# Attention over heads of 16: tiles taken three at a time on rings of three PSUM banks, two banks per instruction

## The reference

```python
x_n = layer_norm(x)
q, k, v = x_n @ Wq + bq, src @ Wk + bk, src @ Wv + bv   # src: x_n or the context
s = einsum('bqhd,bkhd->bhqk', q, k) * 16 ** -0.5 (+ mask)
x = x + (softmax(s) @ v).reshape(b, n, 256) @ Wo + bo
```

## Time and profile before

| what | value |
|---|---|
| median of 3 runs | 4270.73 us (4268.64 to 4275.31) |
| profiled execution, its time and span | 4268.74 us, 4267.0 us |
| PE busy (modelled) | 3949.2 us, 93% |
| DVE, ACT, POOL busy | 2756.7 us (65%), 2414.2 us (57%), 1660.3 us (39%) |
| mean granted clock of PE | 0.944 |
| rough places of the stages, us | SELF0 to 660, CROSS0 to 1110, MLP0 to 1400, CROSS1 to 1860, SELF2 to 2455, CROSS2 to 2960, MLP2 to 3250, SELF3 to the end |

### The profile page before, as it was taken

One profiled execution on the slowest core, in us unless ns is written; L12 is line 12 of the kernel. 1 busy time (PEld: TensorE's weight loads), 2 busy tenths in 40 slices (PEclk: granted clock), 3 DMA queues, 4 the chain that ended last, 5 costly groups with the idle time before them and its releaser, 6 DMA issues. The chain is left out here.

```text
span 4267.0 us, 64410 instructions
## 1 busy us (share of the span) xinstructions
PE 3949.2 (93%) x20562; PEld 1985.0 (47%) x20562; DVE 2756.7 (65%) x6815; ACT 2414.2 (57%) x5093; POOL 1660.3 (39%) x1661
## 2 busy tenths in 40 slices
PE   6988999999796999999999999997988999999998
PEld 3333343333485343333333333432874555555555
DVE  3555568777365777789999978873653444444443
ACT  2444446767431566778888767774324554554553
POOL 2323322111232022137777722211326665666664
PEclk7888889999797899999999999997999999999999
DMA  4434335544001445444444355541000000000000
GB/s 94 85 61 70 62 65 105 82 82 69 24 1 26 103 79 83 76 72 85 61 62 61 57 98 86 81 77 46 1 25 6 6 11 12 11 1 12 11 6 10
DMA packets 135498, 220.30 MB, mean 52 GB/s; under 512 B 42736, under 2 KB 45168, under 8 KB 133488
## 3 DMA queue, kind: packets, MB, share of 16 engines
q1 hardware_dynamic: 135152, 216.02, 28.5%
HBM read 59.69 MB, written 5.51 MB: 15 GB/s over the span
## 5 line engine op out<-in xcount | busy, mean ns | idle before, releaser
L998 ACT ACTIVATE Pr<-ST 128x512 f32<-128x512 f32 (+3 forms) x2220 | 1157.1, 560 | 787.8 <-PE ST L547 774.0
L547 PE MATMUL ST<-stk 50*128 50x512 f32 (+3 forms) x2560 | 1006.6, 456 | 104.5 <-ACT Pr L998 75.8
L1211 DVE TENSOR_REDUCE mx<-MX 128x1 f32<-128x512 f32 x1056 | 701.3, 682 | 259.2 <-PE MX L547 257.1
L547 PE MATMUL MX<-stk 48*128 48x512 f32 (+3 forms) x1760 | 735.1, 455 | 27.6 <-issue 13.6
L1607 POOL TENSOR_SCALAR Pr<-Pr,mx 128x128 f32<-128x128 f32 (+3 forms) x512 | 549.6, 1086 | 388.9 <-DVE mx L1375 388.9
L547 PE MATMUL OV<-Pr,V 128*32 128x512 f32 (+3 forms) x4784 | 633.7, 603 | 2.9 <-ACT Pr L998 1.5
L547 PEld LDWEIGHTS MX<-stk 48*128 48x128 f32 x1760 | 313.5, 192 | 563.6 <-DVE mx L1211 257.1
L547 PEld LDWEIGHTS ST<-stk 50*128 50x128 f32 x2560 | 422.4, 191 | 286.7 <-ACT Pr L998 214.0
L1486 POOL CAST mhl<-mx 128x16 fp32r<-128x16 f32 x160 | 32.1, 201 | 899.2 <-DVE mx L1211 860.6
L1211 DVE TENSOR_REDUCE mx<-OV 128x1 f32<-128x512 f32 x480 | 327.4, 682 | 59.3 <-PE OV L547 58.3
L547 PE MATMUL OV<-stk 48*128 48x512 f32 (+3 forms) x800 | 355.3, 444 | 0.1
(11 more groups left out here) (154 smaller groups left out, 7464.9 us busy)
## 6 DMA issues: line engine op xcount, KB each, us to landing
stk<-hi SPq DMA_DIRECT2D x640, 128.0 KB, 4.8
stk<-lo SPq DMA_DIRECT2D x320, 128.0 KB, 5.4
misc<-misc SPq DMA_DIRECT2D x160, 128.0 KB
sums<-spread SPq DMA_DIRECT2D x80, 256.0 KB
misc<-in_ctx_t SPq DMA_DIRECT2D x24, 512.0 KB, 6.9
W_even<-in_w SPq DMA_DIRECT2D x4, 1024.0 KB, 5.2
W_even<-in_w SPq DMA_DIRECT2D x2, 2048.0 KB, 9.7
XH<-in_ctx_rows SPq DMA_DIRECT2D x8, 512.0 KB, 3.8
```

Source lines behind the costliest of these rows:

```text
L547: return nc.tensor.matmul(o, l, r, start=start, stop=stop)
L998: nc.scalar.activation(pr_buffer(s, u, i)[:, h, q0:S], ST[h % 2][:, q0:S], ACT.Copy if addmask else ACT.Exp).then_inc(ex_done, 2 if addmas ...
L1211: nc.vector.tensor_reduce(m, bank[:, :], AX.X, ALU.max).then_inc(mx_red, 1)
```

## The change

**Runs of three.** The 32 tiles of a pass are numbered k = 0 to 31 and go in eleven runs, ten of three tiles and one of two. PE does the maximum and score tiles of a run, then what is due after that run, by tables.

**Banks.** Maxima and scores each get a ring of three neighbouring banks, so a score tile now waits for the tile three before it. `OUT` takes the products with v. One bank, `L`, takes all other products of an attention layer, one after another: each job waits until the bank has been read out by ACT or DVE (`begin`). The two other layer kinds get their old number of banks under new names.

**Two banks per instruction.** In the cross layers DVE reduces the first tile of a run alone and the other two by one instruction. ACT does the same with exponents (in SELF0 only where both tiles belong to one step; in SELF2 not at all).

**Step buffers.** Exponents go to four step buffers (`prob`, 16 tiles) in all layers, and `values(i)` is placed later, after runs 2, 3, 4, 6, 8, 9, 10 and the next unit's run 0.

**Moves.** LayerNorm's statistics stand after runs 0 to 3 on DVE, the combination after run 3, while the order on POOL is as before. The low parts are taken in runs 4 and 6, after the first maximum there. The first transpose (T0) moves to the end of the slot before.

```diff
+RING = 3
+TILES = 8 * G
+RUNS = [range(k, min(k + RING, TILES)) for k in range(0, TILES, RING)]
+VALUES = {False: {2: 0, 3: 1, 4: 2, 6: 3, 8: 4, 9: 5, 10: 6}, True: {3: 0, 4: 1, 6: 2, 7: 3, 9: 4, 10: 5}}
+TAIL = {False: {0: 7}, True: {0: 6, 1: 7}}
+FIRST_OUT, LAST_OUT = {False: 6, True: 7}, {False: 0, True: 1}
...
-        MX = [pb("MX0"), pb("MX1")]
-        ST = [pb("ST0"), pb("ST1")]
-        OV = [pb("OV0"), pb("OV1")]
-        LA = pb("LA")
-        LB = pb("LB")
+        MXT = es.enter_context(nc.psum_tensor("MX", [P, RING, 512], F32))
+        STT = es.enter_context(nc.psum_tensor("ST", [P, RING, 512], F32))
+        OUT, L = pb("OUT"), pb("L")
...
+        def groups(r, one):
+
+            run = list(RUNS[r])
+            if one(run[-2]):
+                return [run[:-2], run[-2:]] if len(run) == RING else [run]
+            return [[k] for k in run]
```

In PE's slot:

```diff
+                    for r, run in enumerate(RUNS):
+                        for k in run:
...
+                            if on["m"]:
+                                max_tile(ATTN[m_of(s, u)][1], U + 1, 1 - half, k)
+                            if on["b"]:
+                                score_tile(U, half, k)
+                        if on["tail"] and r in TAIL[ATTN[tail_s][2]]:
+                            values(tail_s, U - 1, 1 - half, par if half else 1 - par, TAIL[ATTN[tail_s][2]][r])
+                        if on["b"] and r in VALUES[lag]:
+                            values(s, U, half, par, VALUES[lag][r])
...
+                        if on["b"] and r == (2 if lag else 1):
+                            begin(u, "M1")
+                            turn_max(U, half, 1)
...
+                        if on["a"] and r == 5:
+                            begin(u, "Q")
...
+                        if half == 1 and on["a"] and r == 6:
+                            begin(u, "V0")
...
+                        if on["m"] and r == 7:
+                            begin(u, "M0")
+                            turn_max(U + 1, 1 - half, 0)
...
+                def begin(u, name):
+
+                    wait(pe, l_free, L_NO[s, u, name])
...
+                    wait(pe, mx_red, TILES * (U if k >= RING else U - 1) + before(k) + 1)
```

In ACT's `exp_tiles`:

```diff
+                    wait(act, pv_done, 8 * U + i - 3)
+                    act.wait_ge(st_full, at + n_k)
+                    nc.scalar.activation(prob[:, k % 16:k % 16 + n_k, q0:S], STT[:, k % RING:k % RING + n_k, q0:S],
+                                         ACT.Copy if addmask else ACT.Exp).then_inc(ex_done, 2 if addmask else n_k)
```

In DVE's slot and `max_tiles`:

```diff
+                    for r in range(len(RUNS)):
+                        for tiles in groups(r, lambda k: plain):
...
+                            if on["m"]:
+                                max_tiles(m_of(s, u), U + 1, 1 - half, tiles)
+                            for k in tiles:
+                                if on["b"] and addmask and k % G in BY_VECTOR:
+                                    add_mask(u, U, k)
+                            if on["a"] and r in (4, 6) and tiles[0] == RUNS[r][0]:
+                                low_part(sa, U, half, (r - 4) // 2)
+                        if u != -2 and norm is not None and r < 4:
...
+                            statistics(NB * sn + bn, xt(bn, r), r)
+                            if r == 3:
                                 combine(NB * sn + bn)
...
-                        nc.vector.tensor_reduce(m, bank[:, :], AX.X, ALU.max).then_inc(mx_red, 1)
+                        nc.vector.tensor_reduce(m, MXT[:, k % RING:k % RING + n_k, :], AX.X, ALU.max).then_inc(mx_red, n_k)
```

More of the change, by code:

```diff
@@ L427, in slot @@
                         for kind in range(2):
-                            stack(U + 1, 1 - half, 1, GB + half, kind)
+                            stack(U + 1, 1 - half, 1, kind)
                     if on["tail"]:
@@ L440, in slot @@
                         for kind in range(2):
-                            stack(U + 2, half, 0, GB + 1, kind)
+                            stack(U + 2, half, 0, kind)
                     if on["m"]:
@@ L694, in values, with score_tile @@
-                def values(s, u, U, half, vpar, i):
-                    _, causal, addmask = ATTN[s]
-                    g, kt = i // 4, i % 4
+                    mm(MXB[k % RING][:, 0:k_n], q, stk[lo_p:lo_p + 3 * HD, 8 + i, 0:k_n]).then_inc(mx_full, 1)
+                def score_tile(U, half, k):
+                    _, causal, _ = ATTN[s]
+                    head, kt, k0 = k // G // 4 * 4 + k % G, k // G % 4, before(k)
+                    sb_, ub = unit(U if k >= RING else U - 1) if U > 0 or k >= RING else (s, 0)
+                    if ATTN[sb_][2] and k0 % G in BY_VECTOR:
+                        pe.wait_ge(st_masked, masked(ub, k0 // G, k0 % G) + 1)
+                    else:
+                        wait(pe, ex_done, TILES * (U if k >= RING else U - 1) + k0 + 1)
+                    lo_p, q0 = 64 * half, P * kt if causal else 0
+                    keys = stk[lo_p:lo_p + ROWS, 8 + head, P * kt:P * kt + P]
+                    mm(STB[k % RING][:, q0:S], keys, stk[lo_p:lo_p + ROWS, head, q0:S]).then_inc(st_full, 1)
@@ L951, in slot @@
                 def slot(u, c, b, p, on):
[L952 removed]
+                    half, U = c % 2, UNITS * n + u
                     sa, _ = a_of(s, u, b)
[L954 to L977 removed]
@@ L1199, in max_tile, with output_sum, max_tiles @@
+                def output_sum(end, job, part):
+                    dve.wait_ge(l_full, job + 1)
+                    add_to_x(end[1], part, Lt, l_free)
+                def max_tiles(sm, U, half, tiles):
                     _, causal, addmask = ATTN[sm]
-                    at = 32 * U + 4 * i + qt
-                    waits(dve, (mx_full, at + 1), apart=addmask or causal)
-                    bank, m = MAXB[(4 * i + qt) % 3], mx[:, half, i // 4, qt, i % 4:i % 4 + 1]
+                    k, n_k = tiles[0], len(tiles)
+                    qt = k % NT
+                    waits(dve, (mx_full, TILES * U + k + n_k), apart=addmask or causal)
+                    bank, m = MXB[k % RING], mx[:, half, k:k + n_k]
```

435 lines of the change are left out of this document (199 added, 236 removed).

## The result

The changed kernel takes **4396.79 us** (median), the kernel before, run beside it, 4273.02: ratio 1.028, 95% interval 1.025 to 1.031. The forecast was 4322 with a range of 4245 to 4385. So the direction was right, and 75 us were not foreseen. The four executions of the changed kernel took 4383.71 to 4404.4 us. The profiled execution has a span of 4394.2 us at a granted clock of 0.937.

The account below looks back on a forecast made before the run. PE was taken to be all but full in CROSS0, DVE to bound SELF2, and nothing to be full in SELF0. Cross +26, SELF2 +47 and SELF0 -20 gave +53 us on 4268.74: 4322 us, range 4245 to 4385.

Parts of the forecast that it names:

- Costed at nothing: DMAs and their issues: All layers: DMA timing priced at zero; moved rows landing 5 us after issue, not 3, would cost SELF0 +18 us.
- (a) to (d): Cross layers, two units: runs of three -1.9, third score bank -2.9, two-bank reductions +5.3, one bank L +0.6; sum +1.1 us.
- (c): Cross layers: two-bank maxima free both banks only at their end, so PE waits 5.3 us per two units.
- SELF2, +5.9 us: SELF2: late combination holds POOL's masks, then ACT and PE, 3.9 us; dry DVE 2; +5.9 us per two units, +47 us.
- SELF0, -2.7 us: SELF0: fewer score waits outweigh `values(1)` starting 4 us late and more breaks; -2.7 us per two units, -20 us in all.
- the clock did not come back in SELF0: Rival, SELF0: fewer waits bring PE's clock back up from 0.87, -60 us, total 4262 us; chance 0.13.
- No DVE waits: Rival, everywhere: DVE keeps ahead of PE, so only shorter breaks and the third score bank count; 4060 us; chance 0.12.
- The clock falls in SELF2: Rival, SELF2: more PE waits drop the clock to 0.87, costing 7.5 us per two units; 4382 us; chance 0.12.
- Pairs save more on DVE: Rival, cross layers: 22 two-bank maxima save 0.15 us each, not 0.07; at most -43 us, 4279 us; chance 0.04.

Follow-up runs that it names:

- e6: Changed kernel with SyncE's move of the `product_out` rows issued ahead of the six stack DMAs, nothing moved on DVE; 4317.65 us.
- e5: Changed kernel with the norm's combination two tile groups earlier on DVE and the reciprocal one group later, except in SELF2, where it stays; 4268.5 us.
- e2: Changed kernel with the norm's statistics and combination earlier on DVE, the combination by two tile groups; -73 us against the changed kernel.
- e1: Changed kernel with the reciprocal of the moved rows two tile groups later on DVE; 4347 us.
- e3: Changed kernel with one bank per maximum on DVE in the cross layers, exponents still paired; -24 us against it (-40 by the ratio).
- e8: As e5, with single maxima, POOL's three norm parts one mask step later each, and half 1's output sum behind the first maximum; 4235.5 us, ratio 0.991.
- e10: As e8, with one bank per exponent on ACT in the cross layers too; 4223 us.
- e11: As e10, with SELF2's first product with v one tile group later, in front of the second and apart from the projection of K; 4207.4 us, ratio 0.984.
- e7: Kernel before, with the reciprocal (not in SELF2) three tiles earlier and the combination later, banks and single maxima kept; +139 us against the kernel before.

## Why the prediction was right in sign and wrong in size

**The step that failed** is the sentence "Costed at nothing: DMAs and their issues", and in it: "the few moved rows after `product_out` are issued at 4 us and needed by DVE at 7 to 8, which is close: if they land 5 us after issue rather than 3, SELF0 loses its gain (+18 us in all)". The case that it sets aside is the one that happened: the rows were there 4.4 and 5.4 us after their issue, and the issue itself stood behind six DMAs of 0.6 us. In the half 1 slot above, run 0 starts on DVE at 832.48, so the rows are issued at 5.8 us of the slot and not at 4, DVE is ready for them at 7.1, and has them at 10.2. And the price was set for one layer of four. For SELF0, +18 us was near (e6 gives back 14 there, and e5 is 21.5 below e2). For the cross layers, where the same instruction stands at the same place, it had nothing. There DVE waited 1.78 and 3.08 us in two units; the sum had +1.1 us per two units, and 4.6 were measured (59.6 to 64.2 as the mean of the three layers). e6, which takes this wait away, runs at 4317.65 us, **4 us from the 4322 of the prediction**. So the late rows are, within what the measurements tell, the 75 us that were missing. That the rest comes within 4 us is partly luck: against the kernel before, e6 has -29 us in SELF0 (forecast -20), +39 in the cross layers (+26), +48 in SELF2 (+47) and -9 elsewhere (nothing). The terms:

- *Cross, (a) to (d), +1.1 us per two units.* With the rows in time +2.1 (e6: 61.8 as the mean of the three layers). Runs and the third score bank did what was written: waits of score tiles for ACT fell from 75.8 to 20.2 us in the whole trace.
- *(c), +5.3 us.* The mechanism stood in the trace at its places: in the slot of e1 whose run 5 is shown, the waits before runs 2, 5 and 8 are 0.63, 0.77 and 0.63 us (0.8, 0.85 and 0.8 forecast for half 1), and a reduction over two banks lasts 1.23 us (1.22 forecast). In sum the waits of PE for DVE are 30.9 us in CROSS0 of e6, 4.0 per two units. But the forecast read the 5.3 us as the price of the pairs. Taking them away gave 1.0 us (e3), though the waits named so all but went (e8): PE's tiles then stand one by one for DVE's start every 0.61 us, in part within rows of modelled length. In the two slots compared under e10 the grouping in runs of three makes most of the wait, and the pair its last 0.3 us.
- *SELF2, +5.9 us: 3.9 for POOL's chain and 2 for DVE running dry.* Measured 7.9 (71.7 to 79.6). The weights were the wrong way round. The chain was there link by link, POOL 9.52 us, ACT 6.60, but it costs 2.3 us (e2), since half of it passes under PE's stretch of product and K. The rest, 5.6 us where 2 were put down to dry DVE, is what is left after that. Of it e11 took back 2.7 by moving one product by one run, so that much is shown to be PE's stretch; the cause of the other 2.9 stays open. The lower clock is part of it in a measure that was not separated (product and K are 1.06 and 1.98 us long at the full clock and 1.90 and 2.81 in the slot above).
- *SELF0, -2.7 us.* Measured -2.5 (68.2 to 65.7), but as the difference of two larger terms. The new ring and runs are worth -11.9 us per two units (e5: 56.3), the late combination takes back 6.2 of them (e2: 59.5) and the late rows the other 3.2. I had let `values(1)` be 4 us late, where PE waited 7.6 (60.7 us in 8 waits), and had the score waits for ACT go from 14.3 to 11.0 us; in the layer they went from 42.6 us in all to 2.5. The layer's granted clock of 0.88 in the changed kernel and 0.95 in e5 (window 95 to 550 us) says that the clock pays too when the gap goes. So -2.5 beside -2.7 is luck: two terms, each several times what was put down, that nearly cancel.

A small slip besides: 8 times -2.7 is -22 us, and the sum took -20.

**The rivals.** In the changed kernel the clock did not come back in SELF0 (0.88 against 0.86 before), only when the combination was early: e5's 458.3 us for the layer is 87 below the kernel before, more than the 60 of that rival. *No DVE waits* did not happen, for the reason given. *The clock falls in SELF2* happened in part: 0.91 against 0.95 before, beside 28 us more of busy PE. The Trainium skill, "TensorE: Matmul & The Clock Gate", section "A second HAM failure mode: psum-queue depth-cycling", describes such brief idling between groups as a cause of a swinging clock. This case's rows agree in kind, in the cross layers too, see below. *Pairs save more on DVE* is out: undoing them made nothing slower (e3).

## What to carry to other kernels

A regrouping moves every side job that hangs on the loop's indices. Here two of them, a reciprocal three tiles earlier and a combination seven tiles later, cost as much as the whole change (e7: +139 us in the old kernel), setting them right alone made the loss of 2.8% vanish (e5), and five smaller edits besides, two of which take the instructions over two banks back out of the cross layers, made a gain of 1.6% of it (e11). So list for each moved instruction what it waits for, its DMA's place in the queue included, and who is queued behind it on its engine; and when two numbers of such a check lie a few us apart, price the bad case at every layer in which it can occur.

In a kernel bound by one engine, subtract its busy time from the layer's length before and after, and look at the longest single waits of that engine: they name places to try. Only an edit there shows the cause; one such place (POOL's 9.52 us in SELF2) was worth 18 us, and another (PE's stretch behind run 3) 19.

Compare stages and not only sums: e5 and the kernel before take the same time, and differ by 87, 46 and 39 us in their layers.

## What the runs showed of the hardware

Small transfers behind large ones. An 8 KB DMA issued behind six of 128 KB could be read 4.4 and 5.4 us after its issue, DVE waiting for it. Issued ahead of them (e6) it was read 4.2 us after its issue in the slot shown, and 2.5 to 2.6 us after in most slots of SELF0, without a wait. The queue's 3.9 us (833.31 to 837.23) were saved besides.

The clock can fall inside a dense layer with only short waits of PE in sight. PE in CROSS0 of the changed kernel:

```profile
835.28 0.60 PE L750 MATMUL L<-ident,mhl 128*8 128x128 f32 x4 [0.19 <-DVE X L1190]
...
837.01 0.49 PE L599 MATMUL MX<-stk 48*128 48x512 f32 x1 [0.64 <-DVE mx L1255]
...
837.86 1.94 PE L599 MATMUL OUT<-prob,V 128*32 128x512 f32 x8
839.72 1.65 PE L599 MATMUL L<-misc,W_odd 128*128 128x512 f32 x2
```

The granted clock is 1.00 from 825 to 837 us, 0.50 from 837.8 to 839.7, and 1.00 again from 841.4. The product takes 1.94 us in it, instead of 1.06 at 2.4 GHz, and the half of K 1.65 instead of 1.12: 1.4 us together. Before it stand waits of 0.19 and 0.64 us. They are not enough to name the cause: in the slot of e1 whose run 5 is shown above, waits of 0.19, 0.63, 0.77 and 0.63 us stand in the same places, and the clock stays at 1.00.

That is the step by which the periods of the cross layers differ. In CROSS0 of e6 the granted clock is 1.00 from 620 to 1030 us, and nearly every pair of units takes 61.6 us; in that of e1 it falls once, at 881, and the pair round it takes 63.3 instead of 61.6. In e8 most pairs take 60.8 us, and some 62.1 to 62.4 or 63.7. From 627 to 1100 us of the changed kernel it is 0.97, against 1.00 in the same layer before (620 to 1070), so part of what the late rows cost there came by way of the clock. It may also be why gains from waits taken away don't add to the microsecond.
